# Second attention of a four-stage kernel: the products with the values in three blocks a pair of heads, and row maxima alternating with scores

## What is computed

```python
def _L1_xattn_ref(queries, keys, values, wq_w, wq_b, wk_w, wk_b, wv_w, wv_b, mk, mv, wo_w, wo_b):
    H, DK, DV = (16, 64, 64)
    MEM = 128
    q = (queries @ wq_w + wq_b).reshape(B, S, H, DK).transpose(0, 2, 1, 3)
    k_ext = jnp.concatenate([keys @ wk_w + wk_b, broadcast(mk)], axis=1)
    v_ext = jnp.concatenate([values @ wv_w + wv_b, broadcast(mv)], axis=1)
    ...
    scores = jnp.einsum('bhsd,bhtd->bhst', q, k) / jnp.sqrt(jnp.float32(DK))
    attn = jax.nn.softmax(scores, axis=-1)
    out = jnp.einsum('bhst,bhtd->bhsd', attn, v)
    out = out.transpose(0, 2, 1, 3).reshape(B, S, H * DV)
    return out @ wo_w + wo_b

x = x + _L1_xattn_ref(_layernorm(x), ctx_1024, ctx_1024, ...)
```

## Time and profile before

| | |
|---|---|
| median of 3 runs | 1744.32 us |
| profiled execution, its own time | 1748.7 us |
| its span, first to last instruction | 1747.0 us |
| granted TensorE clock, mean | 0.923 |
| TensorE matmul busy, whole span | 1492.1 us (85%) |
| VectorE, ScalarE, GpSimd busy | 52%, 28%, 26% |
| the 32 pairs of the second attention | about 870 to 1570 us |

### The profile page before, as it was taken

The page is one execution under the profiler, slowest core; times in us unless marked ns, Lnnn a source line. Parts: engine busy times, 40 slices in busy tenths (PEclk is TensorE's granted clock), DMA queues, the critical chain, the costliest instruction groups (busy, mean ns, idle before and its releaser), DMA issues. The chain is left out here.

```text
span 1747.0 us, 18982 instructions
## 1 busy us (share of the span) xinstructions
PE 1492.1 (85%) x6088; PEld 884.1 (51%) x6088; DVE 904.9 (52%) x1684; ACT 494.4 (28%) x618; POOL 450.9 (26%) x257
## 2 busy tenths in 40 slices
PE   5889788898744988995599999999999999977886
PEld 2334334343344777782244446444554455535775
DVE  5556575665440000002557665766566655645666
ACT  2433333334211222220033332333233333320221
POOL 2000000000033000004044443445244533562333
PEclk7889899999956999997599999999999999986998
DMA  6521123202047454425466663565546653402001
GB/s 154 136 38 22 27 36 48 36 9 29 1 165 228 179 189 161 158 72 105 82 82 77 89 80 49 73 85 73 72 60 92 77 73 51 59 0 100 1 1 48
DMA packets 62237, 136.14 MB, mean 78 GB/s; under 512 B 10592, under 2 KB 21216, under 8 KB 57568
## 3 DMA queue, kind: packets, MB, share of 16 engines
q1 hardware_dynamic: 59440, 127.26, 39.1%
q0 software_dynamic: 2736, 8.13, 1.4%
HBM read 58.55 MB, written 12.06 MB: 40 GB/s over the span
## 5 line engine op out<-in xcount | busy, mean ns | idle before, releaser
L1063 POOL TENSOR_TENSOR a_probs<-a_probs 128x1024 f32<-128x1024 f32 x128 | 304.1, 2376 | 415.2 <-PE a_p_os L1626 414.7
L1134 ACT ACTIVATE a_probs<-a_p_s 128x1024 f32<-128x1024 f32 x160 | 163.8, 1023 | 378.5 <-PE a_p_s L1612 378.5
L417 DVE CUSTOM_DVE_ANT_0 a_scratch<-a_p_m,a_bias_q 128x512 bf16<-128x512 f32 x256 | 163.8, 687 | 117.8 <-PE a_p_m L572 117.8
L1345 DVE TENSOR_REDUCE a_max_ctx<-a_p_m 128x1 f32<-128x512 f32 x256 | 169.7, 687 | 79.6 <-PE a_p_m L1587 76.5
L327 ACT ACTIVATE a_probs<-a_p_s 128x1024 f32<-128x1024 f32 x128 | 130.6, 1024 | 175.2 <-PE a_p_s L597 174.7
L595 PE MATMUL a_p_s<-a_q_stack,a_k_stack 128*128 128x512 f32 x256 | 121.2, 500 | 28.5 <-DMA a_q_stack<-a_neg_max 28.5
L572 PE MATMUL a_p_m<-a_k_stack,a_q_stack 127*128 127x512 f32 x256 | 130.4, 555 | 13.6 <-DVE a_mx L417 7.0
L1626 PE MATMUL a_p_os<-a_probs,a_v 128*64 128x512 f32 x512 | 138.1, 618 | 0.0
L1507 PE MATMUL a_p_s<-a_o_raw,a_w 128*128 128x256 f32 x480 | 124.0, 393 | 13.8 <-DVE a_o_raw L1276 13.8
L1587 PE MATMUL a_p_m<-a_k_hl,a_q_hh 128*128 128x512 f32 x256 | 111.1, 481 | 18.3 <-DVE a_v L1323 8.1
L1281 DVE TENSOR_TENSOR a_yb<-a_p_os,a_yb 128x512 f32<-128x512 f32 x15 | 10.4, 691 | 219.1 <-PE a_p_os L1516 219.1
(11 more groups left out here) (200 smaller groups left out, 2135.9 us busy)
## 6 DMA issues: line engine op xcount, KB each, us to landing
a_w<-in_L_w SPq DMA_DIRECT2D x30, 1024.0 KB, 7.8
a_q_hh<-a_hi SPq DMA_DIRECT2D x64, 256.0 KB, 5.7
a_k_hl<-a_hi SPq DMA_DIRECT2D x32, 256.0 KB, 8.0
a_k_hl<-a_lo SPq DMA_DIRECT2D x32, 256.0 KB, 9.5
a_k_h<-a_hi SPq DMA_DIRECT2D x32, 256.0 KB, 10.6
a_q_lm<-a_lo SPq DMA_DIRECT2D x32, 256.0 KB, 7.1
a_ctx_t<-in_ctx_t SPq DMA_DIRECT2D x8, 512.0 KB, 5.6
a_q_stack<-a_hi SPq DMA_DIRECT2D x32, 128.0 KB, 4.8
```

The source lines that it names most:

```text
L417: dve.tensor_tensor_reduce(scratch[:, fill.n % M_BANKS, :], m, bias_q[:, i % NT, :], 1.0, -3.0e38, ALU.add, ALU.max, mx[:, i:i + 1]).then_ ...
L1063: pool.tensor_tensor(probs[:, kt], probs[:, kt - 1], probs[:, kt], ALU.add)\
L1134: act.activation(probs[:, kt, :, :], p_s[:, (KT1 * p + kt) % 2, :, :], ACT.Exp).then_inc(exp_done.sem, 1)
L1345: dve.tensor_reduce(max_ctx[:, NT * head + t:NT * head + t + 1], m, AX, ALU.max)\
```

## The change

The table is rewritten. The products with the values now stand in three places of a pair: tiles 3 and 4 of the pair before at kt = 0, tiles 0 and 1 at kt = 2, tile 2 at kt = 3 (`BLOCKS`). The maxima and `value` no longer stand in twos beside two scores but alternate with them. `normalize` gets a word of its own, at the place where VectorE did it before. `score` waits for the exponentials of two tiles back in the first two tiles of a turn too.

```diff
-                 ("out", "score", "score", "value", "maximum", "maximum", "times_v", "maximum"),
-                 ("out", "maximum", "score", "score", "maximum", "value", "times_v", "maximum"),
-                 ("out", "maximum", "score", "score", "maximum", "times_v", "maximum", "rows"),
-                 ("out", "maximum", "total", "score", "turn", "score", "times_v"))
+                 ("out", "score", "maximum", "value", "maximum", "score", "maximum"),
+                 ("out", "maximum", "score", "value", "maximum", "score", "maximum", "times_v"),
+                 ("out", "maximum", "score", "maximum", "score", "rows", "maximum", "times_v"),
+                 ("out", "maximum", "total", "score", "turn", "score", "normalize"))
+        BLOCKS = {0: (3, 4), 2: (0, 1), 3: (2,)}
...
-                            if what == "times_v" and kt == 4 and (p or behind):
+                            if what == "normalize" and (p or behind):
                                 normalize(b, p - 1)
...
-                if n >= 2 and i == 0:
+                if i == 0:
                     exp_done.wait(pe, b, n - 1)
...
                             elif what == "times_v" and kt:
-                                times_v(b, p, kt - 1)
+                                for k in BLOCKS[kt]:
+                                    times_v(b, p, k)
                             elif what == "times_v" and (p or behind):
-                                times_v(b, p - 1, KT1 - 1)
+                                for k in BLOCKS[kt]:
+                                    times_v(b, p - 1, k)
...
                 if not ahead:
-                    times_v(b, PAIRS - 1, KT1 - 1)
+                    for k in BLOCKS[0]:
+                        times_v(b, PAIRS - 1, k)
```

## The result

The kernel after the change takes 1758.38 us (median of 4 runs, 1756.06 to 1760.09), the kernel before 1745.06 us (1743.05 to 1746.4). The ratio is 1.0079, with an interval of 1.0066 to 1.0092: it became slower by 0.8%. The profiled execution after took 1756.06 us, with a span of 1754.4 us and a mean granted clock of 0.921; before it was 1748.7 us, 1747.0 us and 0.923. The profiled execution after is the lowest of its four, the one before the highest, so the two traces differ by 7.4 us where the medians differ by 13.3.

The account below looks back on a forecast made before the run. The prediction took TensorE's matmul stream as the bound. Even pairs at -8.6 us, odd ones at +4.1 and small terms summed to -3.5 us, from 1744.32 to 1740.8 us, range 1730 to 1750 us.

Parts of the forecast that it names:

- in pair 3 of turns 0 to 2 VectorE's norm statistics stand ahead of the splits, which now end after M0 is due: +0.24 us: Pair 3 of turns 0 to 2: splits end after the pair's first maximum is due, +0.24 us each, +0.7 in the sum.
- the bias add is shut out by GpSimd's add: Rival, even pairs: VectorE's bias add of the values waits for GpSimd's add, +18 us, 1759 us; chance 0.07.
- there is no lower clock to win back: Second attention: TensorE's granted clock already stands at 0.99 to 1.00, so only holes in its stream count.
- Merged blocks: Products with the values: two touching blocks take 1.86 us; tiles 0 and 1 save 0.26, tiles 3 and 4 0.34 us.
- M2 and M3: Third and fourth maximum of a pair: waits for their banks lose 0.69 us in odd pairs, 0.70 in even ones.
- rival of smaller waits: Rival: third and fourth maximum wait less than counted; halved 1731 us, none 1721 us; chance 0.22.
- The turn: Turn of the maxima: starts 3.62 us after tile 2's products, through GpSimd's add and the join; even pairs at 15.19 us.
- The periods: Length of a pair: odd pairs +0.34 us, to 18.7 us; even pairs -0.57 us, to 22.1 us.
- The ends of turns: Three ends of a turn: TensorE waits for the negated maxima, no longer hidden by tile 3's products, +0.25 us each.
- The output pairs: Pair 1 of turns 1 to 3: output projections cover the join before and after, +0.1 us each.
- Pairs 6 and 7 of turn 3: Last two pairs, without maxima: gain 0.6 us each less what the final adds hide, -1.0 us.

Follow-up runs that it names:

- e1_eps_gpsimd: The kernel after the change, with the add of EPS to the variances (L1302) moved from VectorE to GpSimd: 1743.27 us, ratio to before 0.9994.
- e3_before_eps_gpsimd: Control: the kernel before the change, with the add of EPS to the variances moved from VectorE to GpSimd: 1740.41 us, ratio 0.9979.

## Why the prediction was wrong

**The step that failed.** It is the term of the sum "in pair 3 of turns 0 to 2 VectorE's norm statistics stand ahead of the splits, which now end after M0 is due: +0.24 us". Pair 3 became 2.4, 5.5 and 3.8 us longer, 11.7 us in all. Of these 1.0 are the 0.34 us that the sum had for each as an odd pair, so the term measured 10.7 us where the sum had 0.7, and 10.7 us are also what `e1_eps_gpsimd` took back. The wait for L1302 is 1.72 us three times (5.2 us), the lower clock behind it 3.4 and 1.7 us. The statistics as such cost nothing: with L1302 gone and all the rest ahead of the splits, pair 3 is like any odd pair. I had seen that the norm stands there and that its cover had gone, and priced it with durations of the trace before. I had not asked which GpSimd instruction would now run beside each operation of VectorE in that row, as I had done for the values' bias add, 2 us further on. The join of the earlier trace rows had shown that a short VectorE operation can last as long as the add beside it, and L1302 has no operand in PSUM, as the join has none.

The measured 1758.38 us stand beside the 1759 us of the rival *the bias add is shut out by GpSimd's add*. That is chance. Its mechanism did occur, but at another instruction and in three pairs instead of 15; the bias add was never longer, as shown below.

On this the Trainium skill (SBUF, "Who interferes with whom") has a second part that I had left out. It exempts a VectorE instruction with at most one SBUF input only outside the two-port modes; copies and tensor-scalar operations, with one input only, can enter such a mode, which takes the port pair shared with GpSimd, and then whoever is second waits for the whole instruction of the other. This trace agrees: 2.25, 2.08 and 2.08 us instead of 0.17, each to the end of the add. Which mode L1302 ran in, no run shows.

Behind the wait came a second price that the sum did not have. The prediction set out with "there is no lower clock to win back". That was nearly so: in the windows of the earlier trace rows the clock was down at one place, behind the wait of 1.63 us at the jump (0.73 over 5 us), and the 0.99 there comes from it. What the sum lacked is that a new hole can lose the clock: 0.60 in 8.6 us after the wait of 1.72 us in turn 1.

**What held.** TensorE in an even pair of turn 2 and the odd one behind it:

```profile
1368.82 1.08 PE L1627 MATMUL a_p_os<-a_probs,a_v 128*64 128x512 f32 x4
...
1370.69 0.50 PE L1612 MATMUL a_p_s<-a_q_hh,a_k_hl 128*128 128x512 f32 x1
...
1373.68 0.40 PE L1613 MATMUL a_p_s<-a_q_lm,a_k_h 65*128 65x512 f32 x1
1374.17 1.09 PE L1588 MATMUL a_p_m<-a_k_hl,a_q_hh 128*128 128x512 f32 x2
1375.10 0.40 PE L1612 MATMUL a_p_s<-a_q_hh,a_k_hl 128*128 128x512 f32 x1
...
1382.38 1.08 PE L1627 MATMUL a_p_os<-a_probs,a_v 128*64 128x512 f32 x4
...
1385.99 0.27 PE L1598 MATMUL a_p_m<-a_ident,a_mx 128*8 128x128 f32 x1 [0.26 <-DVE a_mx L1355]
...
1394.18 0.39 PE L1613 MATMUL a_p_s<-a_q_lm,a_k_h 65*128 65x512 f32 x1
1394.65 1.10 PE L1588 MATMUL a_p_m<-a_k_hl,a_q_hh 128*128 128x512 f32 x2
1395.59 0.39 PE L1612 MATMUL a_p_s<-a_q_hh,a_k_hl 128*128 128x512 f32 x1
```

- *Merged blocks.* From 1368.82 to 1370.69 are 1.87 us; 1.86 was predicted.
- *M2 and M3.* A score's last matmul takes 0.235 us of TensorE, so in the odd pair M2 is due at 1394.41, and 1395.59 - 1394.41 - 0.47 = 0.71 us are lost (predicted 0.69). In the even pair it is 1375.10 - 1373.91 - 0.47 = 0.72 us (0.70), with M2 loaded 3.48 us behind the score (3.47). The rival of smaller waits is refuted for the steady pairs.
- *The turn* starts 3.61 us behind tile 2 (1382.38 to 1385.99; predicted 3.62) and, in the even pair, 15.30 us behind the first score (15.19).
- *The bias add* was not shut out. 13 of the 32 started while an add of GpSimd ran, and none of the 32 lasted over 693 ns. That rival is refuted too.

```profile
L1324 DVE TENSOR_TENSOR a_v<-a_p_m,a_bv x32: 681/692/693, 792.0 to 1514.2; 128x512 f32<-128x512 f32 x32
```

- *The periods.* Odd pairs take 18.6 us (18.67 predicted), even ones 22.2 us (22.12). Against before that is +0.32 us odd (+0.34) and -0.47 us even (-0.57).
- *The ends of turns*, +0.25 us: two of them show it (-0.22 us where other even pairs have -0.47). The third is the jump back.

**Terms that were mis-sized**, in the trace after against before. The output pairs are 0.64, 0.64 and 0.41 us longer (+0.1 predicted), of which the even pair behind each makes 0.15 us good (-0.72 instead of -0.57 us). Pairs 6 and 7 of turn 3, which have no maxima, win 1.1 us (1.0 predicted). Pair 5 of turn 3 became 1.45 us longer instead of 0.34, and this looks like a second shut-out, though no experiment took it away: the multiplication of `normalize`, whose two inputs are both in SBUF, ran into GpSimd's adds of tiles 3 and 4 and took 1.87 us. 28 of its 32 executions took 0.69 us, and in the kernel before this one, at 1519.71, took 0.93. TensorE then waited 1.28 us for the bank of M2 (VectorE, GpSimd, TensorE):

```profile
1526.71 1.87 DVE L1372 TENSOR_TENSOR a_o_norm<-a_o_raw,a_recip 128x512 f32<-128x512 f32 x1
...
1525.66 5.15 POOL L1064 TENSOR_TENSOR a_probs<-a_probs 128x1024 f32<-128x1024 f32 x2 [3.00 <-PE a_p_os L1627]
...
1529.24 1.09 PE L1588 MATMUL a_p_m<-a_k_hl,a_q_hh 128*128 128x512 f32 x2 [1.28 <-DVE a_max_ctx L1346]
```

All terms outside the three pairs 3 come to 2.0 us more than the sum had for them: -3.2 instead of -5.2 us.

**What stays open.** The forecast was missed by 17.6 us. The traces place 12.0 of these in the pairs, 10.0 in pair 3 and 2.0 in the others; 5.6 us remain. Of the 15.1 us between the medians of the kernel after and `e1_eps_gpsimd`, 9.6 lie in the attention; of the 13.3 us between the two traces, 2.3 lie ahead of the first sums and 1.4 behind the last, and the part ahead varies from 901.07 to 906.95 us over the ten traces of this case. How often the clock falls in pair 3 in runs without a profile isn't known. The other three runs of the kernel after have a mean clock of 0.918 to 0.919, its profiled one 0.921: 0.002 to 0.003 of 1757 us are an estimated 3.5 to 5 us, the size of what is missing, but where they were lost isn't shown. Whether VectorE's pause at the jump comes from fetching its instructions was not tried.

## What to carry to other kernels

When the order on one engine moves, write down for every engine which instruction will now run beside which, also for those of four numbers: a VectorE instruction over 128x4 numbers waited 2 us for GpSimd here, and the engine that bounds the kernel waited for it. A merge of blocks saves its changes of shape, but it takes away cover; keep the merges that cost no wait (tiles 3 and 4) and leave the blocks that stand between two uses of the same bank. A gain of 0.5 us a pair in the bulk is easily lost in the few pairs with extra work, so go through those by row, and look at the clock behind each new hole (here they were of 1.4 to 2.4 us).

## What was not expected of the hardware

- VectorE's sum of 128x4 numbers, with input and output in SBUF, lasted 2.08 to 2.26 us beside an add of GpSimd, and 0.17 us without one, in two kernels.
- TensorE's granted clock fell from 1.00 to 0.60 and 0.51 behind waits of 1.72 and 1.41 us, but not behind each such wait: after the same 1.72 us it was 1.00 in turn 0 and 0.81 in turn 2. A longer wait can leave it up: at the jump of the kernel after TensorE waited 2.44 us, and the clock was 1.00 in the 7.9 us behind.
- Where VectorE's loop over the turns jumps back, the engine rests for 4.57 us (before) and 4.86 us (after) with nothing to wait for:

```profile
1222.72 0.69 DVE L1372 TENSOR_TENSOR a_o_norm<-a_o_raw,a_recip 128x512 f32<-128x512 f32 x1
...
1228.27 1.41 DVE L1337 SCALAR_TENSOR_TENSOR a_lo<-a_p_m,a_bqk,a_hi 128x512 fp32r<-128x512 f32 x2 [4.86 <-issue]
```

  In `e3_before_eps_gpsimd`, with one instruction fewer in the body, the pause fell elsewhere, and the kernel was 0.2% faster; in `e1_eps_gpsimd` the same edit brought nothing there.
